# Third spline convolution: the shifts' table as loaded weights, the one-hots streamed

## What is computed

```python
h = jax.nn.elu(spline_conv(h, row, col, basis, idx, stn1_w, stn1_b))
h = jax.nn.elu(spline_conv(h, row, col, basis, idx, stn2_w, stn2_b))
h = jax.nn.elu(h @ stn3_w + stn3_b)
t = h @ stn4_w + stn4_b
new_pseudo = jnp.clip(pseudo + t[col] - t[row], 0.0, 1.0)
basis2, idx2 = spline_basis(new_pseudo)
return spline_conv(x, row, col, basis2, idx2, conv_w, conv_b)
```

## Time and profile before

| | us |
|---|---|
| median of 3 timed runs | 11127.0 (11125.73 to 11129.64) |
| span of the profiled execution | 14339.7 |
| third convolution in it, first to last product | 8602 to 11975 |

### The profile page before, as it was taken

One profiled execution on the slowest core, in us unless ns is written; L12 is line 12 of the kernel. 1 busy time (PEld: TensorE's weight loads), 2 busy tenths in 40 slices (PEclk: granted clock), 3 DMA queues, 4 the chain that ended last, 5 costly groups with the idle time before them and its releaser, 6 DMA issues. The chain is left out here.

```text
span 14339.7 us, 414245 instructions
## 1 busy us (share of the span) xinstructions
PE 10087.9 (70%) x156361; PEld 8506.1 (59%) x156362; DVE 7530.8 (53%) x18528; ACT 4613.2 (32%) x11707; POOL 6070.4 (42%) x5974
## 2 busy tenths in 40 slices
PE   7566666657366666666677757777787776888888
PEld 7556555546244444444565545666666665888887
DVE  6667666757333333333344434444444444777776
ACT  0001000035122222222233322222222224777776
POOL 0477777743455545455433314444444441111111
PEclk6555555555566666666777767777777776555555
DMA  0222223310222222222211111111111112444443
GB/s 32 45 62 67 64 62 64 64 31 8 76 74 74 74 74 75 74 74 74 69 42 48 42 27 37 35 36 36 35 36 36 34 36 57 115 116 116 115 115 91
DMA packets 850556, 875.92 MB, mean 61 GB/s; under 512 B 629005, under 2 KB 632517, under 8 KB 849966
## 3 DMA queue, kind: packets, MB, share of 16 engines
q1 hardware_dynamic: 622830, 526.55, 13.2%
q0 software_dynamic: 227648, 348.32, 9.9%
HBM read 631.25 MB, written 135.27 MB: 53 GB/s over the span
## 5 line engine op out<-in xcount | busy, mean ns | idle before, releaser
L1611 PE MATMUL c_py<-c_products,c_weights 125*64 125x128 f32 x18944 | 1630.8, 302 | 675.0 <-issue 669.7
L769 POOL DMA_INDIRECT edges_by_rank<-rank_stage,rank_idx x1568 | 1844.7, 1176 | 602.0 <-issue 575.0
L1883 POOL DMA_INDIRECT edges_b<-c_send_rows,c_send_idx x1184 | 1277.9, 1079 | 1902.8 <-DMA c_send_idx<-edge_idx 1586.7
L1556 ACT ACTIVATE c_products<-c_pa 125x512 f32<-125x512 f32 x2368 | 1222.8, 602 | 2391.5 <-remote 1424.9
L1600 PE MATMUL c_pa<-c_near_apart,c_basis 32*125 32x128 f32 x18944 | 1247.0, 315 | 983.2 <-issue 734.5
L1611 PEld LDWEIGHTS c_py<-c_products,c_weights 125*64 125x64 f32 x18944 | 1236.6, 150 | 982.9 <-issue 927.2
L1431 POOL DMA_INDIRECT c_near_ranked<-h_rows,c_idx x1568 | 1597.9, 1019 | 478.1 <-issue 477.8
L1516 DVE TENSOR_TENSOR c_basis<-c_outer,c_hats 128x1000 f32<-128x1000 f32 x296 | 355.4, 1201 | 2745.9 <-PE c_pa L1600 2229.3
L1600 PEld LDWEIGHTS c_pa<-c_near_apart,c_basis 32*125 32x125 f32 x18944 | 958.5, 208 | 1297.4 <-issue 1295.7
L2042 ACT ACTIVATE c_products<-c_pa 125x256 f32<-125x256 f32 x2368 | 713.9, 386 | 2275.5 <-PE c_pa L2125 1411.0
L2125 PE MATMUL c_pa<-c_near_apart,c_basis 32*125 32x128 f32 x18944 | 1180.9, 334 | 242.7 <-issue 201.3
(11 more groups left out here) (402 smaller groups left out, 21318.8 us busy)
## 6 DMA issues: line engine op xcount, KB each, us to landing
rows<-local_rows POOLq DMA_DIRECT2D x548, 256.0 KB, 4.1
own_d<-hparts SPq DMA_DIRECT2D x2192, 48.0 KB, 2.9
hi_rows_in<-hi_rows SPq DMA_DIRECT2D x392, 256.0 KB
c_dst_rows_in<-dst_rows SPq DMA_DIRECT2D x148, 512.0 KB
near_by_rank<-c_near_ranked SPq DMA_DIRECT2D x98, 768.0 KB
rows_both<-hi_rows SPq DMA_DIRECT2D x196, 196.0 KB
near_h<-c_near_h SPq DMA_DIRECT2D x74, 512.0 KB
c_near<-near_h SPq DMA_DIRECT2D x148, 256.0 KB, 2.7
```

The costliest lines, as they stand in the source:

```text
L769: pool.indirect_dma_start(g.ranked, bass.IndirectOffsetOnAxis(idx[:, r, q:q + 1], 0), stage[:, r, q, :], None, bounds_check=last_rank, oob ...
L1556: last = act.activation(by_round[:, half, r, rnd], pa[0:K3, r, 0:TR * P].rearrange("p (f e) -> p f e", f=width), ACT.Copy)
L1611: last = pe.matmul(py[n * width:(n + 1) * width, 0:P], weights[:, f, :], outer[:, half, f, :], start=(f < KP), stop=(f >= width - KP))
L1883: pool.indirect_dma_start(g.edges_b, bass.IndirectOffsetOnAxis(sending.idx[:, n, q:q + 1], 0), sending.rows[:, n, q, :], None, bounds_chec ...
```

## The change

The node number is split at 512 instead of 256: four low blocks (`LOW`) and 13 high parts (`HB`). The table of shifts becomes the loaded weight, 128 rows by 13 x 3 parts x 3 coordinates = 117 columns (`TROW`) for each low block, and the low one-hots of a round's four tiles, 512 columns, are streamed. The result has the slots along the columns; `choose` multiplies it by a one-hot of the high part that now stands along the lanes, and writes bf16. The sum over high parts and bf16 parts is 16 small matmuls on TensorE (`coordinates`), whose weights are the chosen products. The high numbers of the slots are loaded along with the low ones; for that the end of `first_conv` turns and stores both. `move` goes to the start of the next chunk, `take_own` and `spread` to the chunk's end, fold and node sums one round later, `make_outer` of the second half before the node sums' addition. The outer products stream their 64 columns once. The diff, with the places that only repeat a name or a size left out:

```diff
@@ -59,7 +59,10 @@
 STEP = 8
 DEEP = 4
 ND1 = NBLK * P // DST_SB + 1
-HB = NBLK // 2
+LOW = 4
+HB = NBLK // LOW
+TROW = HB * 9
+assert NBLK % LOW == 0 and TROW <= P and LOW * P <= 512
 STEPS = ET // STEP
 EARLY = STEPS // DEEP // 4 * DEEP
...
@@ -226,8 +229,7 @@
             sort_edges(g, c, x, src, dst, attr, wt)
         recycle()
         g.edges = sb("slot_edges", [P, NTS + 2 * CH, ROW_W], F32)
-        g.dst_hi = sb("dst_hi", [P, NTS], F16)
-        g.tparts = sb("t_parts", [P, 3, 2, 3 * HB], BF16)
+        g.tparts = sb("t_parts", [P, LOW, HB, 3, 3], BF16)
         with ExitStack() as c1:
             first_conv(g, c1, stn1_w, stn1_b)
         with ExitStack() as c1:
...
@@ -1268,7 +1271,9 @@
                     n = min(P, NTS - m * P)
                     if m >= 2:
                         pe.wait_ge(s_turn16, m - 1)
-                    pe.transpose(pd[0:n, m % 2, 0:P], low[:, m * P:m * P + n], g.ident[:, :]).then_inc(s_turn, 1)
+                    pe.transpose(pd[0:n, m % 2, 0:P], low_high[:, 0, m * P:m * P + n], g.ident[:, :])
+                    pe.transpose(pd[0:n, m % 2, P:2 * P], low_high[:, 1, m * P:m * P + n],
+                                 g.ident[:, :]).then_inc(s_turn, 1)
 
             @block.scalar
             def _(act):
...
@@ -1758,8 +1764,8 @@
                 st.do(dve.tensor_tensor(t[:, :, 0:3], pf[:, 0:NBLK * 3].rearrange("p (b f) -> p b f", f=3),
                                         b4[:, :].unsqueeze(1).to_broadcast([P, NBLK, 3]), ALU.add))
                 dve.sem_inc(s_ht, 1)
-                split_parts(dve, st, [g.tparts[:, k, :, :].rearrange("p b (h d) -> p b h d", d=3) for k in range(3)],
-                            t[:, :, 0:3].rearrange("p (h b) d -> p b h d", b=2), rest[:, :, :, :])
+                split_parts(dve, st, [g.tparts[:, :, :, k, :] for k in range(3)],
+                            t[:, :, 0:3].rearrange("p (h b) d -> p b h d", b=LOW), rest[:, :, :, :])
 
 
 def third_conv(g, c, x, w_dram):
...
@@ -1790,10 +1795,11 @@
     own_idx = sb("own_idx", [P, DEEP], U32)
     own, own_wide, own_pos = sb("own_shift", [P, 2, 4]), sb("own_wide", [P, CH, 3]), sb("own_pos", [P, CH, 3])
     in_tile, of_group = sb("in_tile", [P, CH]), sb("of_group", [P, P])
-    rows = sb("dst_rows_in", [P, 2, CH * P], F16)
-    hot_lo = sb("dst_hot", [P, 2, 2, CH * P], BF16)
-    hot_hi, num_hi = sb("dst_hot_hi", [P, 2, CH, HB], F16), sb("dst_num_hi", [P, CH, HB], F16)
-    chosen, moved = sb("t_chosen", [P, CH, HB, 3]), sb("t_of_dst", [P, CH, 3])
+    rows = sb("dst_rows_in", [P, 2, 2, CH * P], F16)
+    hot_lo, hot_hi = sb("dst_hot", [P, 2, LOW, CH * P], BF16), sb("dst_hot_hi", [P, 2, CH * P], BF16)
+    high, third, lane_i = sb("dst_high_of_lane", [P, 1]), sb("third_of_lane", [P, 1]), sb("lane_i", [P, 2], I32)
+    coord = sb("coordinate_of_lane", [P, 3], BF16)
+    chosen = sb("t_chosen", [P, CH * P], BF16)
     s_w, s_set, s_dve = sm("w"), sm("set"), sm("dve")
     s_x = sm("x_again")
     s_back, s_row, s_own = ([sm(f"{n}{h}") for h in range(2)] for n in ("near_in", "dst_rows", "own_shifts_sent"))
...
@@ -1836,8 +1843,8 @@
             sp.dma_start(g.x[0:REST, FULL_BLK, :], x[FULL_BLK * P:N, :]).then_inc(s_x, 16)
 
             def dst_rows(k, half):
-                sp.dma_start(rows[:, half, :], g.dst_rows[ds(k * CH, CH), :].rearrange("t e -> (t e)").unsqueeze(0)
-                             .to_broadcast([P, CH * P])).then_inc(s_row[half], 16)
+                sp.dma_start(rows[:, half, :, :], g.dst_rows[:, ds(k * CH, CH), :].rearrange("k t e -> k (t e)")
+                             .unsqueeze(0).to_broadcast([P, 2, CH * P])).then_inc(s_row[half], 16)
 
             def four_chunks(i, last):
                 for n in range(DEEP):
...
@@ -1922,28 +1935,22 @@
             def dst_hots(k, half, filled):
                 dve.wait_ge(s_row[half], filled * 16)
                 dve.wait_ge(s_got, k * ROUNDS + 4)
-                for b in range(2):
-                    dve.tensor_scalar(hot_lo[:, half, b, :], rows[:, half, :], g.nodecol[:, b:b + 1], None, ALU.is_equal)
-                dve.tensor_tensor(hot_hi[:, half, :, :], num_hi[:, :, :],
-                                  g.dst_hi[:, ds(k * CH, CH)].unsqueeze(2).to_broadcast([P, CH, HB]),
+                for b in range(LOW):
+                    dve.tensor_scalar(hot_lo[:, half, b, :], rows[:, half, 0, :], g.nodecol[:, b:b + 1], None, ALU.is_equal)
+                dve.tensor_scalar(hot_hi[:, half, :], rows[:, half, 1, :], high[:, :], None,
                                   ALU.is_equal).then_inc(s_dst, 1)
 
             def choose(k, half, rnd):
                 dve.wait_ge(s_dst, k + 1)
                 dve.wait_ge(s_got, k * ROUNDS + (rnd + 1 + 2 * ROUNDS))
-                tiles = slice(rnd * TR, (rnd + 1) * TR)
-                dve.tensor_tensor(chosen[:, tiles, :, :].rearrange("p j h d -> p (j h) d"),
-                                  pt[:, rnd % 2, 0:TR * HB * 3].rearrange("p (n d) -> p n d", d=3),
-                                  hot_hi[:, half, tiles, :].rearrange("p j h -> p (j h)").unsqueeze(2)
-                                  .to_broadcast([P, TR * HB, 3]), ALU.mult).then_inc(s_chosen, 1)
+                slots = slice(rnd * TR * P, (rnd + 1) * TR * P)
+                dve.tensor_tensor(chosen[0:TROW, slots], pt[0:TROW, rnd % 2, :], hot_hi[0:TROW, half, slots],
+                                  ALU.mult).then_inc(s_chosen, 1)
 
             def move(k, half):
-                dve.wait_ge(s_chosen, k * ROUNDS + (ROUNDS + 2))
-                dve.tensor_reduce(moved[:, :, :], chosen[:, :, :, :].rearrange("p t h d -> p t d h"), AX,
-                                  ALU.add).then_inc(s_sum, 1)
                 dve.wait_ge(s_sum, k + 1)
                 dve.wait_ge(s_hats, k + 1)
-                dve.tensor_tensor(pos[:, half, :, :], g.edges[:, ds(k * CH, CH), 0:3], moved[:, :, :],
+                dve.tensor_tensor(pos[:, half, :, :], g.edges[:, ds(k * CH, CH), 0:3], moved.rearrange("p (t d) -> p t d", d=3),
                                   ALU.add).then_inc(s_moved, 1)
                 dve.wait_ge(s_moved, k * 2 + 1)
                 dve.wait_ge(s_taken, k + 2)
@@ -1993,6 +2000,8 @@
 
             def chunk(i, half, first, left):
                 k = i * 2 + half
+                if left >= 2 and not first:
+                    move(k + 2, half)
                 if left >= 3:
                     choose(k + 3, 1 - half, 0)
                 if left >= 4:
@@ -2002,22 +2011,21 @@
                     make_basis(k + 2, half, i + 2, 0)
                 if left >= 3:
                     choose(k + 3, 1 - half, 1)
+                if left >= 2:
+                    make_outer(k + 2, half, 1)
                 if not first:
                     add(k - 1)
                 dve.tensor_scalar(hot[:, :], g.iotaf[:, 0:2 * P], g.node_in[:, ds(k, 1)], None,
                                   ALU.is_equal).then_inc(s_hot, 1)
                 if left >= 3:
                     own_shifts(k + 3, 1 - half, i + 2 + half)
-                if left >= 2:
-                    make_outer(k + 2, half, 1)
                 if left >= 3:
                     choose(k + 3, 1 - half, 2)
-                    take_own(k + 3)
                 if left >= 2:
                     make_basis(k + 2, half, i + 2, 1)
                 if left >= 3:
                     choose(k + 3, 1 - half, 3)
-                    move(k + 3, 1 - half)
+                    take_own(k + 3)
 
             dst_hots(0, 0, 1)
             for k in range(3):
@@ -2040,7 +2048,7 @@
                 act.wait_ge(s_outer, k * ROUNDS + (rnd + 1 + 2 * ROUNDS))
                 for r in range(4):
                     last = act.activation(by_round[:, half, r, rnd],
-                                          pa[0:K3, r, 0:TR * P].rearrange("p (e f i) -> p e f i", e=REP, f=F)[:, 0],
+                                          pa[0:K3, r, 0:TR * 2 * F].rearrange("p (f i) -> p f i", f=F),
                                           ACT.Copy)
                 last.then_inc(s_kept, 1)
 
@@ -2069,7 +2077,7 @@
                 for rnd in range(ROUNDS):
                     if left >= 1:
                         keep(k + 1, 1 - half, rnd)
-                    if rnd == 0 and not first:
+                    if rnd == 1 and not first:
                         keep_out(k - 1)
                     if rnd == 0 and left >= 2:
                         make_hats(k + 2, half)
@@ -2099,13 +2107,22 @@
                     pe.wait_ge(s_dst, k + 1)
                 pe.wait_ge(s_chosen, k * ROUNDS + (rnd + 1))
                 pe.sem_inc(s_pe_turn, 1)
-                for j in range(TR):
-                    t = rnd * TR + j
-                    for n in range(6):
-                        last = pe.matmul(pt[:, rnd % 2, j * 3 * HB:(j + 1) * 3 * HB],
-                                         hot_lo[:, half, n // 3, t * P:(t + 1) * P], g.tparts[:, n % 3, n // 3, :],
```

(42 more changed lines are left out.)

34 lines of the change are left out of this document (21 added, 13 removed).

## The result

The changed kernel takes 11461.7 us (median of 4 runs, 11450.5 to 11481.3), the kernel before 11127.7 us beside it: ratio 1.0296, 95% interval 1.0284 to 1.0309, 334 us slower. The forecast of 11320 us had the sign, and its upper end of 11450 us lies 12 us under the result; the third rival, the clock, had named 11480 us.

The account below looks back on a forecast made before the run. GpSimd's 12.3 us a chunk was taken as the bound before, a serial VectorE-TensorE loop of 13.6 us after: +1.3 us times 148, +190 us. 11127 + 190 + 5 = about 11320 us, range 11040 to 11450 us.

Parts of the forecast that it names:

- the third rival, the clock: Third convolution: idle TensorE drops to 1.2 GHz, gather and weighing double, 1.1 us more a chunk, 11480 us; chance 10%.
- The ring: Own shifts to VectorE's first product through TensorE's coordinates, weighing, gather: 2.5 us; with the rest 13.6 us a chunk, +190 us.
- the semaphore: Third convolution, between VectorE's own shifts and TensorE's coordinates: 0.1 us for the signal.
- the coordinates: TensorE, third convolution: 16 new small matmuls at 0.035 us each, 0.7 us with the step to the next block.
- the rest of the loop: VectorE, third convolution, first product to own shifts: 8.7 us before, 8.7 + 0.8 + 1.6 = 11.1 us after.
- The chunk of before: Third convolution of the kernel before: 12.3 us a chunk, GpSimd's nine indirect DMAs and the time between them.
- the case of no change: Third convolution: GpSimd bounds, needing 13.6 us a chunk in both kernels because loads come late, 11130 us; chance 13%.
- The outer products' half stream: TensorE, third convolution: streaming 64 instead of 128 columns saves nothing; bound on one side -0.45 us a round.
- One-hots: VectorE, third convolution: three more by tensor_scalar at 0.74 us each, +2.2 us a chunk.
- products: VectorE, third convolution: four a chunk grow from 0.48 to 0.685 us each, +0.8 us; bf16 output given no gain.
- The gather: TensorE, third convolution: 4 matmuls of 512 columns at 0.23 us replace 24 of 78, 0.92 us, the same time.
- The rival of slow issue: Third convolution: slow TensorE issue also occurs in timed runs and fewer matmuls make the kernel faster, 11050 us; chance 23%.

Follow-up runs that it names:

- experiment 3: Changed kernel with chosen products double-buffered, coordinates behind round 0's gather and position steps behind VectorE's first product: 11204.9 us, ratio 1.0056 to the kernel before.
- experiment 7: Changed kernel with chosen products double-buffered, coordinates behind round 0's gather, and outer products streaming 128 columns again: 11171.8 us, ratio 1.0016 to the kernel before.
- experiment 9: Changed kernel with six matmuls, their result overwritten unread, ahead of the coordinates' wait on TensorE: 11349.1 us, ratio 1.0172 to the kernel before.
- experiment 1: Kernel before measured and profiled again with nothing edited: 11117.1 us, profile span 11115.4 us.
- experiment 2: Changed kernel with the outer products streaming 128 columns again: 11379.7 us, ratio 1.0216 to the kernel before.
- experiment 4: Kernel before with the outer products streaming 64 columns once: 11202.5 us, ratio 1.0052 to the kernel before.
- experiment 5: Kernel before with seven instead of eight GpSimd sends a chunk, the rest moved to the second convolution's end: 11270.6 us, ratio 1.0112.
- experiment 12: Kernel before with VectorE making the spread's input and node addition ahead of round 1's product, all eight sends kept: 11191.7 us, ratio 1.0037.

## Why the prediction went wrong

**The ring** was right, and its price came out, in part by luck: it is the difference of two chunks that were both some 0.8 us too short (below). Forecast 2.5 us from the own shifts to the first product, measured 2.58; its terms are less exact than their sum. From the taking of the own shifts to the coordinates it is 0.42 us, where the 0.1 us for the semaphore had no row behind it, and the coordinates take 0.47 us to the next block instead of 0.7. Forecast +1.3 us a chunk over before, measured 14.37 - 13.10 = 1.27 us; forecast +190 us, measured 188. Experiments 3 and 7 show that the order and not the work costs.

**The step that failed is the clock.** I saw it and priced its step, +1.1 us on the ring against 1.34 measured in a long chunk; but I gave it 10% and put it at nothing in the sum, where it measures 139 us. That its time of 11480 us is 18 us from the result is partly luck: I had 1.1 us in every chunk, and measured it is 1.34 us on the ring and 0.63 us in the rest of the loop in every second one. The prediction gives no reason for so low a chance, and its own rows speak against it: they showed the clock at 0.67 in a stretch in which TensorE was starved, and blocks of 1.71 instead of 1.01 us right behind one, and the forecast itself had TensorE idle 1.4 us in every chunk. Measured, 1.96 us of idling are followed by a clock of 0.57 in every second chunk. Experiment 9, in which only that idling is filled, takes back 112 us with more work done.

**The chunk of before** was mis-sized in both terms alike, which hid it. I took 12.3 us, GpSimd's total and the longest of three; it is 13.1 us. My ring came to 13.6 us; it is 14.4. GpSimd's total lacked 0.8 us: somewhat more than half of it are gaps between its DMAs, as the one ahead of a chunk's first send was a wait for loads in the first profile and not in the sum, and the rest is longer DMAs (1.11 us for 1.08, own shifts 1.21 for 1.06). The totals of TensorE and VectorE left out their waits on each other. On TensorE these are the 0.8 and 0.5 us of experiment 1. On VectorE, the rest of the loop was put together from busy time (8.7 + 0.8 + 1.6 = 11.1 us) and is 11.79 us: ahead of the node addition alone VectorE idles 93.1 / 144 = 0.65 us (in the kernel before, with a product in front of the addition, 0.3 us). What it waits for isn't shown; the profile names the instruction before it on VectorE itself. The kernel reads the node block's number into a register of VectorE there, which doesn't count as busy; whether that read takes the time was not tested. The errors cancel in the difference and only there: the case of no change began for me at 13.6 us of GpSimd work, and GpSimd stood at 13.1 us already, half a microsecond from it.

**The outer products' half stream** was taken at nothing with a lower bound of -0.45 us a round. The spacing is indeed the same: 32 matmuls in 1.10 us against 1.15 before, 1.03 and 1.08 us to the next block. But I had no bound on the other side. Experiments 2 and 4 put it at 82 us in the changed kernel, a part of the clock's 139 us and not in addition to it, and at 66 us alone. With the spacing unchanged and the chunks at the full clock as long as before (experiment 4), the clock is what the runs show for it.

**The rest** held. One-hots 0.76 us (0.74), products 0.69 us (0.685); a bf16 result brings the product nothing. The gather takes 1.01 us to the next block, 0.25 us a matmul (0.23); the Trainium skill's 131 ns ("TensorE: Matmul & The Clock Gate", section "Back-to-back issue gap") isn't reached in this loop. **The rival of slow issue** falls with experiment 1: without the recording's disturbance there is none. It was right to leave it out of the sum; 23% was much for time that the timed runs had no room for.

## What to carry to other kernels

When an edit makes TensorE wait for another engine inside a loop, price not the wait alone but also the blocks behind it at 1.2 GHz, and look whether these blocks lie on the ring that made the wait. A step moved from one engine to another can turn serial work into a ring; here a second buffer and a place one block later in both engines' queues took away three quarters of the loss. The pace of a loop is its busy time plus its waits: a sum of busy times is a floor, and where two limits lie level, shortening one of them alone showed no gain (experiments 5 and 12).

## What the runs showed of the hardware that was not expected

TensorE's granted clock fell with less work per instruction. With no wait added, 64 instead of 128 streamed columns in the same number of matmuls at the same spacing took it from 0.99 to 0.95 (experiment 4) and, without the ring, from 1.00 to 0.95 (experiments 7 and 3). Matmuls that do nothing useful brought it from 0.83 to 0.99 and made the kernel 1% faster (experiment 9). A low clock is not a price everywhere: between 1000 and 2900 us, in the sorting, it was 0.50 in the profile of experiment 7 and 1.00 in that of experiment 3, with TensorE busy 1164 and 1161 us and its costliest group of matmuls at 453 and 452 ns. So the mean clock of a whole run doesn't tell its time; the blocks' own durations do.

GpSimd's indirect DMAs get longer beside some of VectorE's work. In the timeline of the kernel before (experiment 1):

```profile
7500.04 1.20 DVE L1978 TENSOR_TENSOR c_basis<-c_outer,c_hats 128x1000 f32<-128x1000 f32 x1 [0.54 <-PE c_pa L2125]
7500.16 1.94 POOL L1883 DMA_INDIRECT edges_b<-c_send_rows,c_send_idx  x1 [0.30 <-issue]
7501.15 0.68 DVE L1982 TENSOR_TENSOR c_near_apart<-c_near,c_real 128x512 f32<-128x512 f32 x1
...
7502.48 1.87 DVE L1942 TENSOR_REDUCE c_t_of_dst<-c_t_chosen 128x48 f32<-128x1248 f32 x1
7503.69 0.98 POOL L1883 DMA_INDIRECT edges_b<-c_send_rows,c_send_idx  x1 [0.30 <-issue]
```

The same instruction takes 0.98 us beside the reduction and 1.94 us beside two products that read both operands from SBUF; it ends 0.27 us after the second of them. From 7200 to 7800 us of that profile all 89 sends that run beside the reduction and beside no product of these and no one-hot take 0.98 us; those beside L1978 or L1982 take up to 1.95. The Trainium skill, "SBUF — State Buffer", section "SBUF: two separate sides", tells that GpSimd can't write a transfer's descriptors while VectorE holds the ports that they share; the trace fits it, with these numbers, though it doesn't show the ports. So GpSimd's 13.1 us a chunk seem to be partly VectorE's doing, and when VectorE has more of such work, GpSimd's pace may slow with it: a send takes 1.11 us on average in the kernel before and 1.16 in experiment 3. That this difference comes from the one-hots was not tested.
